# A selective-scan and mixture-of-experts kernel: the product dt·u·B of each scan step is moved from GpSimd to TensorE, with the decays in SBUF and a new order of the scan stage

## The reference, cut to what matters

```
def step(state, inp):
    d, b, c, u = inp
    dA = jnp.exp(d[..., None] * A)
    state = state * dA + (d * u)[..., None] * b[:, None, :]
    y = jnp.einsum('bdn,bn->bd', state, c)
    return (state, y)
...
y = y + D[None, :, None] * x
y = y * silu(z)
```

## Time and profile before

| what | before |
|---|---|
| median of 3 runs | 1026.5 us (1023.62 to 1029.08) |
| span of the profiled execution | 1028.2 us |
| time of the profiled execution itself | not given apart from its span |
| PE busy | 857.8 us (83%) |
| DVE busy | 602.9 us (59%) |
| POOL busy | 565.6 us (55%) |
| ACT busy | 498.3 us (48%) |
| mean granted TensorE clock | 0.907 of full speed |

### The profile page before, as it was taken

One profiled execution on the slowest core, in us unless ns is written; L12 is line 12 of the kernel. 1 busy time (PEld: TensorE's weight loads), 2 busy tenths in 40 slices (PEclk: granted clock), 3 DMA queues, 4 the chain that ended last, 5 costly groups with the idle time before them and its releaser, 6 DMA issues.

```text
span 1028.2 us, 12633 instructions
## 1 busy us (share of the span) xinstructions
PE 857.8 (83%) x4237; PEld 474.1 (46%) x4237; DVE 602.9 (59%) x862; ACT 498.3 (48%) x895; POOL 565.6 (55%) x318
## 2 busy tenths in 40 slices
PE   6375745668899886999789998999999989989984
PEld 3153544445455464554555574444444443444441
DVE  4489999889989889998798862222122111111111
ACT  3589655697776788766766333222222211212120
POOL 0288998987988988979877601132222222212121
PEclk8568656589899988999899999999999999999997
DMA  8632345334334453332636677999999999999994
GB/s 279 237 123 108 140 141 166 123 123 166 126 125 144 164 167 127 123 123 92 236 105 241 232 261 269 393 391 393 396 386 398 398 397 396 398 386 386 399 385 103
DMA packets 68411, 250.66 MB, mean 244 GB/s; under 512 B 10506, under 2 KB 13078, under 8 KB 68092
## 3 DMA queue, kind: packets, MB, share of 16 engines
q1 hardware_dynamic: 54740, 226.09, 58.2%
q0 software_dynamic: 7712, 18.88, 7.6%
q10 hardware_dynamic: 5896, 4.90, 1.4%
HBM read 230.67 MB, written 19.17 MB: 243 GB/s over the span
## 4 chain that ended last, share of the span: by engine, by line
PE 51%; DVE 16%; DMA 11%; issue 6%; ACT 4%; SPq 3%; POOL 2%; POOLq 0%; ACTq 0%; DVEq 0%
PE ps L687 11%; PE ps L890 11%; PE ps L682 10%; PE ps L698 8%; PE ps L914 6%; DVE ps L1278 5%; DMA arena<-in_L_ffn_w_down 5%; DVE arena L1285 3%; SPq L573 3%; DVE arena L1306 2%; DMA out_rows<-routes,idxs 1%; DMA out_rows<-xn,idxs 1%; DVE arena L1278 1%; PE ps L923 1%; DMA xn_rows<-scores 1%
## 5 line engine op out<-in xcount | busy, mean ns | idle before, releaser
L1524 POOL TENSOR_TENSOR arena<-arena 128x1024 f32<-128x1024 f32 x128 | 300.1, 2362 | 58.1 <-DVE arena L568 41.0
L682 PE MATMUL ps<-ident,arena 128*128 128x128 f32 (+2 forms) x1408 | 232.7, 315 | 89.2 <-DVE ps L1286 40.6
L682 PEld LDWEIGHTS ps<-ident,arena 128*128 128x128 f32 (+2 forms) x1408 | 194.0, 174 | 195.1 <-issue 89.5
L1085 ACT ACTIVATE ps<-arena,An 128x511 f32<-128x511 f32 x256 | 165.3, 680 | 109.0 <-DVE ps L1286 93.7
L1278 DVE TENSOR_TENSOR_SCAN ps<-ps,arena 128x1024 f32<-128x1024 f32 x82 | 187.6, 2288 | 15.0 <-ACT ps L1085 14.2
L890 PE MATMUL ps<-arena 128*64 128x352 f32 x984 | 160.7, 465 | 9.0 <-issue 6.6
L687 PE MATMUL ps<-xnT,sw 128*128 128x512 f32 x320 | 150.4, 614 | 12.7 <-ACT arena L1046 11.8
L1538 POOL DMA_INDIRECT arena<-xn_rows,idu x32 | 34.1, 1067 | 222.5 <-DVE wcol L1434 174.4
L1529 POOL TENSOR_TENSOR arena<-arena 128x1024 f32<-128x1024 f32 x46 | 108.4, 2357 | 47.8 <-DVE arena L1278 44.5
L1441 DVE TENSOR_TENSOR arena<-arena,ps 128x352 f32<-128x352 f32 x32 | 16.7, 522 | 172.2 <-PE ps L890 172.2
L890 PEld LDWEIGHTS ps<-arena 128*64 128x64 f32 x984 | 74.0, 138 | 83.0 <-issue 72.2
(11 more groups left out here) (170 smaller groups left out, 906.2 us busy)
## 6 DMA issues: line engine op xcount, KB each, us to landing
arena<-bc_rows SPq DMA_DIRECT2D x128, 512.0 KB, 4.7
arena<-in_L_ffn_w_down SPq DMA_DIRECT2D x59, 768.0 KB, 23.2
arena<-in_L_ffn_w_gate SPq DMA_DIRECT2D x64, 704.0 KB, 23.5
arena<-in_L_ffn_w_up SPq DMA_DIRECT2D x59, 704.0 KB, 23.5
arena<-in_x SPq DMA_DIRECT2D x4, 1024.0 KB, 7.2
xn_rows<-xn ACTq DMA_DIRECT2D x4, 1024.0 KB, 6.6
out_rows<-arena SPq DMA_DIRECT2D x4, 1024.0 KB, 5.1
extra<-in_L_ffn_w_up SPq DMA_DIRECT2D x5, 704.0 KB, 23.1
```

The costliest lines, as they stand in the source:

```text
L682: return nc.tensor.matmul(dst, src, ident[0:k, 0:k], is_transpose=True, **kw)
L1085: a = nc.scalar.activation(ps[:, 2 * (c % 2) + n, 1:L], dt[k][:, 1:L], ACT.Exp, scale=An[:, k, NB * g + n:NB * g + n + 1])
L1524: G.tensor_tensor(R[c % RING], dtu[k][:, None, :].to_broadcast([P, NB, L]), Brep[n % REPS], ALU.mult)\
```

## The change

The diff changes five things.

1. dt*u of a block is transposed by PE ("dtuT", 4 transpositions) and copied to SBUF by ACT, as lhsT. The B rows of the batch are transposed too ("bT": PE, then ACT into the small tile bT). For each pair of steps POOL makes 8 diagonal 128x128 blocks of B ("diag", one affine_select of 128x1024). For each step PE multiplies the transposed dt*u by these, 8 products of 128x128x128, which writes dt*u*B into the PSUM pair. The broadcasts of B are gone, and with them half of the "rep" loads.
2. The decays go to a ring of 3 SBUF tiles, the outputs R to another ring of 3. The first columns are zeroed once, so L1286 goes.
3. u*D is no longer made by ACT; "duT" multiplies u by a diagonal of D, which DVE makes once (diagD).
4. `by_vector` becomes a set of 27 steps, so 101 of the 128 weighings are POOL's.
5. The order of the whole stage is new, as a table for each step in us. In it the last jobs of the shared unit of batch 2 (sdown) stand behind the last steps, and the store of batch 2 ("sp out") behind pieces 11 to 19 in SP's queue.

```diff
-RING = 5
+DECS = 3
+OUTS = 3
 REPS = 3
+DIAGS = 2
...
+VECTOR = {5, 8, 10, 11, 14, 25, 27, 28, 29, 30, 43, 46, 49, 50, 55, 61, 62, 63, 76, 91, 93, 109, 111, 115, 116, 124,
+    126}
...
         def by_vector(q):
-            return q % 2 == 1 or q in EXTRA
+            return q in VECTOR
...
                     if n >= REPS:
-                        sp.wait_ge(s["dbu_done"], 2 * (n - REPS) + 2)
                         for q in (2 * (n - REPS), 2 * (n - REPS) + 1):
                             weighed(sp, q)
                     g = n % NG
-                    for dst, row in ((Brep, 0), (Crep, NS)):
-                        load(dst[n % REPS], bc_dram[b:b + 1, row + NB * g:row + NB * (g + 1), :].to_broadcast([P, NB, L]),
-                             rep_in[n % REPS])
+                    load(Crep[n % REPS], c_dram[b:b + 1, NB * g:NB * (g + 1), :].to_broadcast([P, NB, L]),
+                         rep_in[n % REPS])
...
                     for t in range(LT):
-                        mm = transpose(ps[:, 4 + c % 2, t * P:(t + 1) * P], du[c % 2][:, t * P:(t + 1) * P],
-                                       start=(t == 0), stop=False, skip_group_check=True)
+                        mm = nc.tensor.matmul(ps[:, 4 + c % 2, t * P:(t + 1) * P], u[c][:, t * P:(t + 1) * P],
+                                              diagD[:, c, :], start=(t == 0), stop=False, skip_group_check=True)
                     mm.then_inc(s["duT_mm"], 1)
+                elif kind == "dtuT":
+                    claim(bank)
+                    pe.wait_ge(s["dtu_ready"], i + 1)
+                    flip(bank, 0, [dtu[c % 2][:, t * P:(t + 1) * P] for t in range(LT)]).then_inc(s["dtuT_mm"], 1)
+                    freed[bank] = [(s["dtuT_ready"], i + 1)]
+                elif kind == "dbu":
+                    k, n = step_of(c)[1], c // 2
+                    pe.wait_ge(s["diag_done"], n + 1)
+                    pe.wait_ge(s["dtuT_ready"], DC * b + k + 1)
+                    if c < 2:
+                        pe.wait_ge(s["pre_ev"], 4)
+                    elif by_vector(c - 2):
+                        pe.wait_ge(s["cs_odd"], vector_weighs(c - 2))
+                    else:
+                        pe.wait_ge(s["scan_done"], c - 1)
+                    for t in range(LT):
+                        for m in range(NB):
+                            mm = nc.tensor.matmul(ps[:, 2 * (c % 2) + m, t * P:(t + 1) * P], dtuT[k][:, t, :],
+                                                  diag[n % DIAGS][:, NB * t + m, :], start=True, stop=True)
+                    mm.then_inc(s["dbu_done"], 1)
...
-                    if c >= 2:
-                        if by_vector(c - 2):
-                            act.wait_ge(s["cs_odd"], vector_weighs(c - 2))
-                        else:
-                            act.wait_ge(s["scan_done"], c - 1)
+                    if c >= DECS:
+                        act.wait_ge(s["scan_done"], c - DECS + 1)
                     for n in range(NB):
-                        a = nc.scalar.activation(ps[:, 2 * (c % 2) + n, 1:L], dt[k][:, 1:L], ACT.Exp,
+                        a = nc.scalar.activation(decay[c % DECS][:, n, 1:L], dt[k][:, 1:L], ACT.Exp,
                                                  scale=An[:, k, NB * g + n:NB * g + n + 1])
...
                     pair = flat(ps[:, 2 * (q % 2):2 * (q % 2) + 2, :])
-                    V.tensor_tensor_scan(pair if by_vector(q) else flat(R[q % RING]), pair, flat(R[q % RING]), 0.0,
+                    V.tensor_tensor_scan(pair if by_vector(q) else flat(R[q % OUTS]), flat(decay[q % DECS]), pair, 0.0,
                                          ALU.mult, ALU.add).then_inc(s["scan_done"], 1)
...
-                    link(V.tensor_tensor(R[q % RING], ps[:, h:h + 2, :], Crep[n % REPS], ALU.mult))
-                    V.memset(ps[:, h + 1, 0:1], 0.0).then_inc(s["cs_odd"], 1)
+                    V.tensor_tensor(R[q % OUTS], ps[:, h:h + 2, :], Crep[n % REPS], ALU.mult).then_inc(s["cs_odd"], 1)
...
-                elif kind == "dbu":
-                    k, n = step_of(c)[1], c // 2
-                    pool.wait_ge(s["dtu_ready"], DC * b + k + 1)
-                    pool.wait_ge(rep_in[n % REPS], 32 * (n // REPS + 1))
-                    if c >= RING:
-                        pool.wait_ge(s["yT_mm"], c - RING + 1)
-                    G.tensor_tensor(R[c % RING], dtu[k][:, None, :].to_broadcast([P, NB, L]), Brep[n % REPS], ALU.mult)\
-                        .then_inc(s["dbu_done"], 1)
+                elif kind == "diag":
+                    n, g = c, c % NG
+                    pool.wait_ge(s["bT_ready"], b + 1)
+                    if n >= DIAGS:
+                        pool.wait_ge(s["dbu_done"], 2 * (n - DIAGS) + 2)
+                    G.affine_select(out=diag[n % DIAGS], in_=bT[:, b % 2, g, :, None].to_broadcast([P, LT * NB, P]),
+                                    compare_op=ALU.is_equal, fill=0.0, base=0, pattern=[[0, LT * NB], [-1, P]],
+                                    channel_multiplier=1).then_inc(s["diag_done"], 1)
```

More of the change, by code:

```diff
@@ L48 @@
 LOWER = -3.3e38
[L54 to L109, removed]
-}
@@ L135 @@
[L135 to L158, removed]
-    "act ssilu": [50.51, 50.67, 51.07, 51.11, 51.13, 51.14],
-    "pe sup": [50.39, 50.83, 51.24, 51.9, 52.08, 52.52, 52.93, 53.35, 53.76, 53.89, 54.65, 55.06],
-    "dve shs": [52.17, 52.99, 53.84, 54.68, 55.54, 56.4],
-    "pe sdown": [57.47, 57.87, 58.3, 58.82, 59.25, 59.4, 59.66, 59.85, 60.29, 61.5, 61.91, 62.35],
-    "dve sdown": [59.06, 61.06, 61.06, 63.12],
-    "sp out": [64.66],
-}
@@ new lines @@
+BANKS = [
+    {
+        "bT": [6],
+        "ctx": [6, 7],
+        "dt": [6, 7, 7, 6],
+        "dtuT": [7, 7, 6, 6],
+        "inproj": [6, 7, 4, 5],
+        "logits": [7],
+        "pos": [7],
+        "sdown": [6, 7, 6, 7],
+        "sgate": [6, 7, 6, 6, 6, 6],
+        "sup": [7, 7, 6, 6, 6, 7],
+        "table": [7],
+        "xdbl": [6],
+        "xnT": [6, 6, 7, 6],
+        "zT": [7, 6, 7, 6],
+    },
+    {
+        "bT": [6],
+        "ctx": [6, 7],
+        "dt": [7, 6, 6, 6],
+        "dtuT": [7, 7, 6, 6],
+        "inproj": [7, 6, 6, 7],
+        "logits": [7],
+        "pos": [6],
+        "sdown": [6, 7, 6, 6],
+        "sgate": [7, 6, 7, 6, 6, 6],
+        "sup": [6, 7, 6, 6, 7, 7],
+        "table": [7],
+        "xdbl": [6],
+        "xnT": [6, 6, 6, 7],
+        "zT": [6, 6, 6, 7],
+    },
+    {
+        "bT": [7],
+        "ctx": [6, 6],
+        "dt": [6, 6, 7, 6],
+        "dtuT": [6, 6, 7, 6],
+        "inproj": [6, 7, 6, 7],
+        "logits": [7],
+        "pos": [7],
+        "sdown": [6, 6, 6, 6],
+        "sgate": [7, 6, 7, 6, 7, 7],
+        "sup": [6, 7, 6, 6, 7, 6],
+        "table": [6],
+        "xdbl": [6],
+        "xnT": [6, 7, 7, 7],
+        "zT": [7, 6, 7, 7],
+    },
+    {
+        "bT": [6],
+        "ctx": [7, 6],
+        "dt": [7, 7, 6, 7],
+        "dtuT": [6, 6, 6, 6],
+        "inproj": [7, 7, 7, 6],
+        "xdbl": [6],
+        "zT": [7, 6, 6, 6],
+        "xnT": [1, 2, 6, 7],
+        "logits": [3],
+        "sgate": [0, 1, 0, 3, 0],
+        "pos": [2],
+        "table": [1],
+        "sel": [7],
+        "warm": [3],
+        "pospre": [2],
+    },
+]
@@ L260, in build @@
+EACH = ['acc', 'c', 'conv', 'ctx', 'dt', 'dtu', 'dtuT', 'duT', 'exp', 'gate', 'inproj', 'ln', 'logits', 'ohsid', 'scopy', 'score', 'sdown', 'sgate', 'shs', 'sp', 'ssilu', 'sup', 'u', 'x2', 'xdt', 'xn', 'xnT', 'xstats', 'zT', 'zs', 'zstats']
 def build(nc, x, ctx_1024, in_proj_w, conv_w, conv_b, x_proj_w, dt_proj_w, dt_proj_b, A_log, D,
           gate_w, w_gate, w_up, w_down, sw_gate, sw_up, sw_down, out):
-    bc_dram = nc.dram_tensor("bc_rows", [B, 2 * NS, L], F32, kind="Internal").ap()
+    c_dram = nc.dram_tensor("c_rows", [B, NS, L], F32, kind="Internal").ap()
@@ L474, in first_phase @@
                                 m = None
[L475 to L480 removed]
+                            BANK[kind, b, m] = BANKS[b][kind][m or 0]
             parts.sort()
@@ L617, in _ @@
                     sp.wait_ge(s["xdbl_ready"], b + 1)
-                    load(bc_dram[b], xdbl[DR:DR + 2 * NS, :], s["bc_st"])
+                    load(c_dram[b], xdbl[DR + NS:DR + 2 * NS, :], s["bc_st"])
                 elif kind == "rep":
```

481 lines of the change are left out of this document (333 added, 148 removed), and 57 rows, old and new, of tables (PAIR, STEP).

## The result

The changed kernel takes **1144.87 us** (median of four runs, 1144.35 to 1146.09) beside 1026.36 for the kernel before on the same chip: a ratio of 1.1143, 95% interval 1.1111 to 1.1175. The forecast was 1119, the range 1069 to 1185. The profiled execution took 1144.79 us with a span of 1143.1; of before the span is 1028.2, so there are 114.9 us to account for.

What follows compares the result with a forecast made beforehand. The prediction took DVE as pacing the kernel at first, DVE and PE later, and PE after the change. The span 1028.2 + 92 from the second stretch gave 1120, less 1.7 to the median: 1119 us, range 1069 to 1185.

Steps and rivals of the forecast that it cites:

- PE needs 600 us in a stage that now lasts 545: Scan stage: PE's 361 us of work plus 239 us new, mostly 128 steps of products at 1.74 us.
- The upper end of 3.04: Price in us of a step's dbu products on PE if weight loads are not hidden; 389 us for 128 steps.
- First stretch, 150 us, no gain: First 39 scans: PE needs 127 us, DVE 119, neither filling the other's gaps; about 150 us for 149.
- the clock rival: PE's clock stays at 0.66 in the first stretch: 192 us for 150, +42, total 1161 us; chance 0.10.
- Second stretch, +92: Other 89 scans: PE needs 473 us and is 97% full, so 488 us for the 396 of before.
- DVE's 67 us hidden: Scan stage: 55 weighings leave DVE, 67 us, hidden under PE's 600; they would show if PE were faster.
- POOL 382 us, ACT, DMA, SP nothing: Scan stage: POOL falls from 471 to 382 us, hidden under PE; ACT, DMA and SP changes cost nothing.
- What follows the scans moves as a block: Last scan to the end, 438 us, mostly weight streaming: taken to shift unchanged.
- What was to be seen: Signs: gapless PE starts, two records a product, DVE about 65%, POOL around 60%, scans waiting for dbu, last scan near 680.
- One inference on the clock: First stretch: if transpositions don't count as clock activity, 1119 stands; if that is wrong, the sum is the clock rival's.
- 1161 + 27: Upper end of the range: the clock case plus 27 us of unhidden weight loads, rounded to 1185.
- The first rival: A 128-column product costs no more than a transposition, 0.87 us a step: stage 42 us shorter, 984 us; chance 0.09.

Runs made afterwards that it cites:

- dbu_twice: The changed kernel with each of the 8 products of a dbu issued twice; single run, 1367.91 us.
- dbu_transposed: The changed kernel with each dbu product replaced by a transposition of the same tile, factor B left out; 1049.8 us, ratio 1.0195 to the kernel before.
- dbu_bf16: The changed kernel with transposed dt*u and the diagonals of B rounded to bf16, one record a product; 1020.59 us, ratio 0.9903 to the kernel before.
- before_pe_load: The kernel before, in its old order, with 8 32-bit products by a zero tile added to each yT group; 1169.04 us, ratio 1.1363.
- old_weighs: The changed kernel with 55 weighings back on DVE, right behind their scans; 1149.82 us, ratio 1.117 to the kernel before.
- bf16_old_weighs: dbu_bf16 with the edits of ctx_late and old_weighs added; 1028.51 us, ratio 1.001 to the kernel before.
- tail_early2: ctx_late with batch 3's layer norm, logits and maxima and the fill transpositions moved ahead, fourth xnT on a free bank; 1130.29 us, ratio 1.0972.
- best_tail2: dbu_bf16 with the edit of ctx_late and the same moves as tail_early2; 1007.84 us, ratio 0.9785 to the kernel before.
- ctx_late: The changed kernel with batch 1's context behind the first dbu jobs and batch 2's context load behind the first broadcasts; 1133.23 us, ratio 1.1007.

## Why the prediction was right, step by step

- **"PE needs 600 us in a stage that now lasts 545", the deciding step: right.** PE is at 99% in the second stretch, and the product's price, taken at 1.74 us from two distant rows, is 1.743 in dbu_twice as a mean and 1.79 from start to start in a single group. The upper end of 3.04 (loads not hidden) is out. The cause is shown from both sides: half the records take off 95 (dbu_transposed) or 124 us (dbu_bf16), the same products alone put 142 on (before_pe_load).
- **First stretch, 150 us, no gain: right** (149.2). Clock 0.97, so the clock rival is out. With a light product the same 40 scans take 133.7 us (dbu_transposed) and 133.4 (dbu_bf16), so it is the products that eat the gain here too.
- **Second stretch, +92: right in sum.** The scans are later by 80.6, and 16 us of PE work that the sum counted come out behind the last scan: 97. Two errors largely cancel in it: PE was busy for 488 us in this stretch, not for the 473 that the count gave, and 99% of the time, not 97.
- **DVE's 67 us hidden: right**, 3 to 5 us in old_weighs. The forecast said that they would show if PE were faster: of them 18 do in bf16_old_weighs.
- **POOL 382 us, ACT, DMA, SP nothing: right.** POOL had 373; a select took 1.10 us for the 1.3 taken.
- **"What follows the scans moves as a block": right from the first gather on** (-1.0), wrong for the 8 us ahead of it: the router of batch 2 was moved behind the last steps, and that move got no price. About 4 of the 8 are shown, by tail_early2 and best_tail2; the rest is open.
- **The front: the step that is missing.** The sum starts at the first scan and takes the 48 us before it as they were. But the new order also moves batch 1's context ahead of xdbl of batch 0 on PE, and this was the place for a sentence on what stands behind a waiting instruction. It is 13.6 us by the profile and 11 to 14 by ctx_late, about half of the 26 by which the forecast was low. 13.6 + 8 + 5 (97 for 92), less 2.5 and 1.0, is 23: a span of 1143 for the 1120 of the sum. The last 3 us lie between span and median: the forecast took the median 1.7 below the span, and it is 1.8 above.
- **What was to be seen** came in the main: starts without gaps, two records a product, DVE at 64% (65), POOL at 58% (60). The scans' idle time ends with PE in place of ACT, but more with the transposing helper (84.1 us) than with the dbu (38.3). The last scan at 682 for 680 is luck: the front made it 13.6 us later, and the 16 us of PE work behind it made it sooner.
- **One inference on the clock fails.** That the sum is the clock rival's if transpositions do count does not follow: in dbu_transposed they do count, and the clock is near full all the same (last section).
- **Slips that changed nothing.** In the earlier trace rows the clock is near full from the ninth slice, not the eighth. 1161 + 27 is 1188, not 1185. The first rival decides from (529 - 377) / 128 = 1.2 us a step on down, not 1.1.

## What to carry to other kernels

Before giving an engine new work, count its records in the stage and price each by the distance between starts: a busy time of 80% with 184 us free was enough to decide this, though the trace had no such product. In an order written out by hand, go through every queue from its first instruction: one job that waits for a DMA, placed ahead of the job that opens the critical chain, cost 12 us that no sum over stages showed. Work moved from an engine is worth its full time only while that engine sets the pace; here 67 us of DVE were worth 3 to 5 with PE full and 18 with PE lighter.
